# Second layer: where each attention row is divided by its mass

## The chip, the cores and the metric

The kernel runs on one NeuronCore of one Trainium2 chip. The metric is the device time of one execution in microseconds (us). Five engines work from queues of their own, each in the order of its program, and meet at semaphores: PE (TensorE, with its weight loads shown apart as PEld), DVE (VectorE), ACT (ScalarE), POOL (GpSimd) and SP (SyncE, which here issues the DMAs).

## What is computed

A graph of 1250 nodes with 512 features and 20000 edges goes through four layers. The second is a transformer of four blocks; each block has sparse attention with four heads of 128 features, written here densely over all 1250 x 1250 pairs with a matrix that holds the logarithm of the number of edges between two nodes, or -1e30 where there is none:

```python
for i in range(NUM_BLOCKS):                       # 4
    y = _cond_layer_norm(x, cond, s1_w[i], s1_b[i], b1_w[i], b1_b[i])
    # q, k, v = three projections of y, 4 heads each
    scores = jnp.einsum('ehd,ehd->eh', q[src], k[dst])
    smax = jax.ops.segment_max(scores, src, num_segments=N)
    ex = jnp.exp(scores - smax[src])
    denom = jax.ops.segment_sum(ex, src, num_segments=N)
    attn = ex / denom[src]
    y = jax.ops.segment_sum(attn[:, :, None] * v[dst], src, num_segments=N) @ wo + bo
    x = x + y
    # a second conditioned norm and a two-layer perceptron, added to x
```

## The kernel before

Nodes lie in 10 tiles of 125 rows. `second_layer` loops over the four blocks; inside, the attention loops over 4 heads and, in each, over steps i = 0 to 11, which hold tile i at one stage and earlier tiles at later ones. Every engine's queue is written out by hand in that loop, so the order of the code is the order of the work. For tile j of a head the stages are:

1. PE, `scores`: nine matmuls give the 125 x 1250 scores in PSUM (three for each of three column cuts, as queries and keys are split into a high and a low part). It waits until DVE has read the tile before (`scored`), since both use the same PSUM banks.
2. DVE, `row_scores` (L790, L794): adds the log counts, writes the row of scores to `prob` (two buffers) and its maximum.
3. ACT (L1248): the exponential in place, with the row sum (`fx.mass`).
4. DVE, `row_mass` (L800, L802): the inverse of the row sum.
5. PE, `turn` (L1087): ten 125 x 125 transposes of `prob` into PSUM in three units. It waits for the exponential (`exped`).
6. ACT (L1245) copies each unit to bf16 (`pt_h`), DVE (L1379) writes the rest of it as a second bf16 part (`pt_l`).
7. POOL (L941) puts the 125 inverse masses on the diagonal of a matrix, PE (`mass_on_rows`, L1096) multiplies it with ones so that every partition holds the inverse masses as a row, and ACT (L1257) copies two tiles of them to SBUF (`mass_rows`).
8. PE, `weighted` (15 matmuls a tile, a group of two tiles accumulating in one PSUM bank, `bank(5)`): values times turned probabilities. Before it starts a group it waits until DVE has read the one before (`o_done`).
9. DVE, `attend` (L1347): product of the group's 128 x 250 result and `mass_rows`.

In step i PE does `scores(i)`, `weighted(i-3)`, `turn(i-1)`, `mass_on_rows(i-2)`; ACT does the three copies of tile i-1 and then the exponential of tile i; DVE does `row_scores(i)`, `row_mass(i-1)`, the three `pt_l` of tile i-1 and, in even steps from 4 on, `attend`. Between two heads PE computes the next head's queries and keys (`project`, six products of 12 matmuls), with `turn(9)` after the first. In the last head of a block there is no next projection; there ACT and DVE also split the earlier heads' results (`attended_high`, `attended_low`, L1352) in steps 2 to 7. After the last `attend` of a block SP loads the block's input back, POOL adds a bias to it (L962) and DVE adds the output projection to it. POOL also splits the head weights (L894, L896) between its diagonals.

## Time and profile before

| | us |
|---|---|
| median of 3 runs | 2759.81 |
| lowest and highest | 2756.35 and 2760.05 |
| the profiled execution | 2755.59 |
| its span | 2753.6 |
| busy in the span: PE, DVE, ACT, POOL | 2383.1, 1724.6, 1009.4, 747.2 |

The span is the time from the first to the last instruction of the profiled execution; 2.0 us lie around it. Busy times are sums over stages with different limits, so the attention has to be read by itself: its first block lies between about 425 and 671 us of the span, and the other three repeat it, which makes about 980 us of the 2754.

### The profile page before, as it was taken

To read this page: it belongs to the slowest core of one execution; us is meant where nothing else is said; L and a number is where in the kernel's file an instruction comes from. 1 tells how busy PE (TensorE), PEld (TensorE's weight loads), DVE (VectorE), ACT (ScalarE), POOL (GpSimd) and SP (SyncE) were. 2 spreads that over 40 slices of the span, in tenths; PEclk is the share of its full clock that TensorE was granted. 3 is DMA by queue.
4 is the path that set the end of the run, shared out by engine and by line. 5 is a ranking of instruction groups with operands and counts; after the bars stand their busy time and mean duration, and the time that the engine had idled before them with its cause. 6 is when DMAs were issued, how large, how long until landed. Compare 5 with 4: busy or idle time off the path is not lost. (4 is left out here: it accounts for less than half of the span.)

```text
span 2753.6 us, 40835 instructions
## 1 busy us (share of the span) xinstructions
PE 2383.1 (87%) x14014; PEld 1794.2 (65%) x14014; DVE 1724.6 (63%) x3212; ACT 1009.4 (37%) x1746; POOL 747.2 (27%) x627
## 2 busy tenths in 40 slices
PE   6889879998888999788999798899987997888783
PEld 6884458887766888576888686788765553333331
DVE  8994355666654666644666655566663335899985
ACT  1123044445334555324555433454530032243342
POOL 0000051212532121533121344111160000366673
PEclk9999989999999999899999998999998997988887
DMA  1013020001101000201000210100024300000000
GB/s 61 30 44 95 22 74 9 9 9 52 41 21 50 9 13 5 86 24 47 9 9 9 68 37 27 36 9 9 24 95 144 81 9 19 0 0 0 1 0 37
DMA packets 67598, 91.20 MB, mean 33 GB/s; under 512 B 20485, under 2 KB 36869, under 8 KB 67377
## 3 DMA queue, kind: packets, MB, share of 16 engines
q1 hardware_dynamic: 67377, 88.41, 10.2%
q8 instruction: 120, 1.97, 0.3%
q14 instruction: 101, 0.83, 0.1%
HBM read 62.94 MB, written 25.45 MB: 32 GB/s over the span
## 5 line engine op out<-in xcount | busy, mean ns | idle before, releaser
L941 POOL TENSOR_SCALAR inverse_mass_diagonal<-identity,row_masses 125x125 f32<-125x125 f32 x160 | 96.8, 605 | 873.0 <-DVE row_masses L802 812.2
L1245 ACT ACTIVATE urned_probabilities_high<-psum 125x500 bf16<-125x500 f32 (+1 forms) x480 | 214.2, 521 | 251.5 <-PE psum L1087 251.5
L1379 DVE TENSOR_TENSOR turned_probabilities_low<-psum,urned_probabilities_high 125x500 bf16<-125x500 f32 (+1 forms) x480 | 254.3, 586 | 81.2 <-ACT urned_probabilities_high L1245 81.2
L790 DVE CUSTOM_DVE_ANT_0 probabilities<-psum,counts 125x1250 f32<-125x1250 f32 x160 | 233.5, 1459 | 103.3 <-PE psum L664 102.6
L1731 POOL TENSOR_TENSOR logs_and_shifts<-logs_by_source,target_spreads 125x1250 f32<-125x1250 f32 x80 | 217.4, 2722 | 156.4 <-DVE probabilities_turned L1804 88.5
L1950 PE MATMUL psum<-probabilities_turned,values_and_ones 125*65 125x512 f32 (+1 forms) x480 | 212.5, 589 | 34.7 <-ACT probabilities_turned L1867 18.6
L1248 ACT ACTIVATE probabilities<-probabilities,row_peaks 125x1250 f32<-125x1250 f32 x160 | 215.6, 1348 | 69.9 <-DVE row_peaks L794 67.9
L662 PE MATMUL psum<-urned_probabilities_high,values_high 125*128 125x250 bf16 x800 | 217.5, 272 | 13.1 <-DVE attended_turned L1347 8.8
L664 PE MATMUL psum<-urned_probabilities_high,values_low 125*128 125x250 bf16 x800 | 215.0, 269 | 0.0
L663 PE MATMUL psum<-turned_probabilities_low,values_high 125*128 125x250 bf16 x800 | 214.7, 268 | 0.0
L1804 DVE SCALAR_TENSOR_TENSOR probabilities_turned<-target_spreads,source_bends,logs_and_shifts 125x1250 f32<-125x1250 f32 x80 | 202.5, 2537 | 18.2 <-POOL logs_and_shifts L1731 18.2
L662 PE MATMUL psum<-keys_high,queries_high 128*125 128x512 f32 (+1 forms) x480 | 183.1, 381 | 28.9 <-DVE row_peaks L790 23.1
L1087 PE MATMUL psum<-identity,probabilities 125*125 125x125 f32 x1600 | 201.4, 273 | 1.3 <-ACT probabilities L1248 1.3
L1087 PEld LDWEIGHTS psum<-identity,probabilities 125*125 125x125 f32 x1600 | 187.9, 188 | 4.5 <-DVE turned_probabilities_low L1379 2.4
L445 ACT ACTIVATE norm_std<-norm_moments,norm_eps 125x1 f32<-125x1 f32 x120 | 35.2, 294 | 406.9 <-DVE norm_moments L441 406.9
L1950 PEld LDWEIGHTS psum<-probabilities_turned,values_and_ones 125*65 125x65 f32 x480 | 68.4, 153 | 172.4 <-issue 140.7
L662 PE MATMUL psum<-turned_high,head_weights 128*128 128x500 f32 (+1 forms) x384 | 145.3, 378 | 33.9 <-DVE queries_low L1339 25.8
L663 PE MATMUL psum<-keys_low,queries_high 128*125 128x512 f32 (+1 forms) x480 | 170.0, 354 | 0.0
L664 PE MATMUL psum<-keys_high,queries_low 128*125 128x512 f32 (+1 forms) x480 | 169.5, 353 | 0.0
L1867 ACT ACTIVATE probabilities_turned<-probabilities_turned,score_columns 125x1250 f32<-125x1250 f32 x80 | 106.7, 1337 | 156.3 <-DVE probabilities_turned L1804 156.0
L662 PE MATMUL psum<-slot_b_high,turned_high 128*125 128x512 f32 x320 | 134.4, 420 | 30.8 <-DVE nodes L1395 18.2
L306 PE MATMUL psum<-onehot_band,onehot_source 125*125 x2200 | 137.5, 224 | 17.2 <-DVE onehot_band L261 16.4
(267 smaller groups left out, 5449.8 us busy)
## 6 DMA issues: line engine op xcount, KB each, us to landing
block_inputs_kept<-nodes SPq DMA_DIRECT2D x4, 2500.0 KB
nodes<-block_inputs_kept SPq DMA_DIRECT2D x8, 1250.0 KB
weight_stage<-in_L_gnn_m_w SPq DMA_DIRECT2D x32, 256.0 KB, 2.6
counts_kept<-counts_by_target_rows SPq DMA_DIRECT2D x10, 625.0 KB, 3.5
counts_by_target<-counts_kept SPq DMA_DIRECT2D x1, 6103.5 KB
logs_kept<-counts SPq DMA_DIRECT2D x1, 5468.8 KB
logs_by_source<-logs_kept SPq DMA_DIRECT2D x1, 4375.0 KB
weight_stage<-in_L_gnn_wv SPq DMA_DIRECT2D x16, 256.0 KB, 2.6
```

The source lines that it names most:

```text
L306: mm = pe.matmul(region(b)[:, k * 128:(k + 1) * 128], onehot[0:TILE, q, k * TILE:(k + 1) * TILE], station[0:TILE, bass.ds(at, 1), q, :, :] ...
L662: pe.matmul(out, lh, rh, start=first, stop=False, skip_group_check=True)
L663: pe.matmul(out, lh, rl, start=False, stop=False, skip_group_check=True)
L664: return pe.matmul(out, ll, rh, start=False, stop=last, skip_group_check=True)
L790: dve.tensor_tensor_reduce(prob[0:TILE, i % 2, :], scores, fx.count_src[0:TILE, i, 0:NODES], scale, MASKED, ALU.add, ALU.max, p[:, 0:1]).t ...
L1087: mm = pe.transpose(bank((3, 4, 7)[u])[0:TILE, cols(d - 4 * u)], prob[0:TILE, j % 2, cols(d)], fx.ident[0:TILE, 0:TILE])
L1245: nc.scalar.activation(dst, src, ACT.Copy).then_inc(pt_high, 1)
L1248: nc.scalar.activation(prob[0:TILE, i % 2, :], prob[0:TILE, i % 2, :], ACT.Exp, bias=fx.peak[0:TILE, i % 2, 1:2], accum_out=fx.mass[0:TILE ...
L1379: dve.tensor_tensor(dst, src, high, ALU.subtract).then_inc(pt_low, 1)
L1731: nc.gpsimd.tensor_tensor(offset[0:TILE, T % 2, :], lw.logs[0:TILE, j, :], shifts[0:TILE, h % 2, :], ALU.add).then_inc(offset_ready, 1)
L1804: dve.scalar_tensor_tensor(prob[0:TILE, T % 4, :], target[0:TILE, h % 2, :], bend[0:TILE, j, h:h + 1], offset[0:TILE, T % 2, :], ALU.max, ...
L1950: mm = pe.matmul(region(0)[0:WIDTH, a:z], values[0:TILE, j, h, :], prob[0:TILE, T % 4, a:z], start=(j == 0), stop=(j == TILES - 1))
```

## The change

In the attention of the second layer the inverse masses no longer travel to the result. DVE multiplies each row of `prob` by its own inverse mass, a number per partition, in place, before the transposes; `turn` waits for that (`scaled`) and not for the exponential. Stage 7 is gone with its buffers and semaphores, `attend` is a plain copy out of PSUM, and on DVE `row_mass(i-1)`, which now has three instructions, stands ahead of `row_scores(i)`.

```diff
@@ row_mass
             dve.reciprocal(m[:, 2:3], m[:, 1:2]).then_inc(inverted, 1)
+            dve.wait_ge(inverted, T + 1)
+            p = prob[0:TILE, i % 2, :]
+            dve.tensor_scalar(p, p, m[:, 2:3], None, ALU.mult).then_inc(scaled, 1)
@@ POOL, steps of a head
-                        if h > 0 or j >= 2:
-
-                            pool.wait_ge(rows_prod, T - 1)
-                        wait_apart(pool, fx, inverted, T + 1)
-                        nc.gpsimd.tensor_scalar(mass_diag[0:TILE, j % 2, :], fx.ident[0:TILE, 0:TILE],
-                                                fx.mass[0:TILE, j, 2:3], None, ALU.mult).then_inc(diagonal, 1)
@@ PE, turn
-                    pe.wait_ge(exped, 40 * b + 10 * h + j + 1)
+                    pe.wait_ge(scaled, 40 * b + 10 * h + j + 1)
@@ PE, steps of a head
-                        if i >= 2:
-                            mass_on_rows(h, i - 2)
@@ ACT, steps of a head
-                        if i >= 3 and i % 2 == 1:
-                            g = (i - 3) // 2
-                            act.wait_ge(rows_prod, 40 * b + 10 * h + 2 * g + 2)
...
-                            nc.scalar.activation(mass_rows[:, g % 2, :], bank(6)[:, 0:250],
-                                                 ACT.Copy).then_inc(rows_copied, 1)
@@ DVE, attend
-                    dve.wait_ge(rows_copied, 20 * b + 5 * h + g + 1)
-                    dve.tensor_tensor(attended[:, h, 250 * g:250 * g + 250], bank(5)[:, 0:250], mass_rows[:, g % 2, :],
-                                      ALU.mult).then_inc(o_done, 1)
+                    dve.tensor_copy(attended[:, h, 250 * g:250 * g + 250], bank(5)[:, 0:250]).then_inc(o_done, 1)
@@ DVE, steps of a head
+                        if 1 <= i <= TILES:
+                            row_mass(dve, i - 1, T - 1)
                         if i < TILES:
...
                             row_scores(dve, psum[0:TILE, 0:NODES], i, T, HDIM1 ** -0.5)
-                        if 1 <= i <= TILES:
-                            row_mass(dve, i - 1, T - 1)
```

The queue of DVE in one even step from the middle of a head, before: the last `pt_l` of a tile, `attend`, and then the next step.

```order
L1379 TENSOR_TENSOR turned_probabilities_low<-psum,turned_probabilities_high 125x2x125
L1347 TENSOR_TENSOR attended_turned<-psum,inverse_mass_rows 128x250
L433 REGISTER_ALU
L790 ISA probabilities,row_peaks<-psum,counts 125x1250
L790 ISA row_peaks 125x1
L794 TENSOR_SCALAR row_peaks<-row_peaks 125x1
L800 TENSOR_SCALAR row_masses<-row_masses 125x1
L802 RECIPROCAL row_masses<-row_masses 125x1
L1376 REGISTER_ALU
L1379 TENSOR_TENSOR turned_probabilities_low<-psum,turned_probabilities_high 125x4x125
```

The same place of DVE's queue with the change (L786 is `row_scores`, L796 to L801 `row_mass`, L1320 `attend`, L1351 `pt_l`):

```order
L1351 TENSOR_TENSOR turned_probabilities_low<-psum,turned_probabilities_high 125x2x125
L1320 COPY attended_turned<-psum 128x250
L796 TENSOR_SCALAR row_masses<-row_masses 125x1
L798 RECIPROCAL row_masses<-row_masses 125x1
L801 TENSOR_SCALAR probabilities<-probabilities,row_masses 125x1250
L433 REGISTER_ALU
L786 ISA probabilities,row_peaks<-psum,counts 125x1250
L786 ISA row_peaks 125x1
L790 TENSOR_SCALAR row_peaks<-row_peaks 125x1
L1348 REGISTER_ALU
L1351 TENSOR_TENSOR turned_probabilities_low<-psum,turned_probabilities_high 125x4x125
```

The two instructions on the masses moved ahead of the scores of the next tile, with the 125 x 1250 product of the row behind them.

The queue of PE at the end of a step before, from the last matmul of `weighted` through `turn` to `scores`:

```order
L664 MATMUL psum<-turned_probabilities_high,values_low 128x250
L1085 REGISTER_ALU
L1087 MATMUL psum<-identity,probabilities 125x125 x4
L1085 REGISTER_ALU
L1087 MATMUL psum<-identity,probabilities 125x125 x4
L1085 REGISTER_ALU
L1087 MATMUL psum<-identity,probabilities 125x125 x2
L1096 MATMUL psum<-inverse_mass_diagonal,all_ones 128x125
L1059 REGISTER_ALU
L662 MATMUL psum<-keys_high,queries_high 125x512
```

And with the change (L1079 is `turn`):

```order
L1077 REGISTER_ALU
L1079 MATMUL psum<-identity,probabilities 125x125 x4
L1077 REGISTER_ALU
L1079 MATMUL psum<-identity,probabilities 125x125 x4
L1077 REGISTER_ALU
L1079 MATMUL psum<-identity,probabilities 125x125 x2
L1051 REGISTER_ALU
L662 MATMUL psum<-keys_high,queries_high 125x512
```

The one product between the transposes and the next scores is gone; nothing else on PE moved.

## Rows read from the trace of the kernel before

**Rows 1.** Stretches: start:end and length, each engine's busy us, granted clock, DMA.
```profile
425.00:671.00 246.00, 234.14 (x1661) 205.33 (x1659) 160.64 (x362) 131.10 (x248) 43.64 (x58) 1.00 0.04 11
```
**Rows 2.** Page, groups of instructions: busy us, mean ns, idle before and its releaser.
```profile
L941 POOL TENSOR_SCALAR inverse_mass_diagonal<-identity,row_masses 125x125 f32<-125x125 f32 x160 | 96.8, 605 | 873.0 <-DVE row_masses L802 812.2
```
**Rows 3.** Timeline of PE, one step of the first head: start us, duration, instruction.
```profile
447.00 0.27 PE L662 MATMUL psum<-urned_probabilities_high,values_high 125*128 125x250 bf16 x1
...
448.61 1.25 PE L1087 MATMUL psum<-identity,probabilities 125*125 125x125 f32 x10
449.70 0.39 PE L1096 MATMUL psum<-inverse_mass_diagonal,all_ones 125*128 125x125 f32 x2
449.84 0.50 PE L662 MATMUL psum<-keys_high,queries_high 128*125 128x512 f32 x1
...
451.70 0.28 PE L662 MATMUL psum<-urned_probabilities_high,values_high 125*128 125x250 bf16 x1
```
**Rows 4.** Timeline of DVE in the same step (idle before and releaser in brackets).
```profile
446.45 0.41 DVE L1347 TENSOR_TENSOR attended_turned<-psum,inverse_mass_rows 128x250 f32<-128x250 f32 x1
447.08 1.46 DVE L790 CUSTOM_DVE_ANT_0 probabilities<-psum,counts 125x1250 f32<-125x1250 f32 x1 [0.22 <-PE psum L664]
...
448.58 0.15 DVE L794 TENSOR_SCALAR row_peaks<-row_peaks 125x1 f32<-125x1 f32 x1
448.65 0.14 DVE L800 TENSOR_SCALAR row_masses<-row_masses 125x1 f32<-125x1 f32 x1
448.83 0.16 DVE L802 RECIPROCAL row_masses<-row_masses 125x1 f32<-125x1 f32 x1
449.87 1.59 DVE L1379 TENSOR_TENSOR turned_probabilities_low<-psum,urned_probabilities_high 125x500 bf16<-125x500 f32 x3 [0.87 <-ACT urned_probabilities_high L1245]
```
**Rows 5.** Timeline of ACT in the same step.
```profile
449.24 1.34 ACT L1245 ACTIVATE urned_probabilities_high<-psum 125x500 bf16<-125x500 f32 x3 [2.27 <-PE psum L1087]
450.45 1.35 ACT L1248 ACTIVATE probabilities<-probabilities,row_peaks 125x1250 f32<-125x1250 f32 x1
451.69 0.21 ACT L1248 ACTIVATION_READ_ACCUMULATOR probabilities<-probabilities,row_peaks 125x1 f32 x1
```
**Rows 6.** One line's instructions: DVE, a product with a number per partition.
```profile
L565 DVE TENSOR_SCALAR noise_phase<-noise_phase,lane_number x1: 864/864/864, 211.7 to 211.7; 64x1250 f32<-64x1250 f32 x1
```
**Rows 7.** Timeline of ACT and PE: the last transposes of a block.
```profile
660.27 0.21 ACT L1248 ACTIVATION_READ_ACCUMULATOR probabilities<-probabilities,row_peaks 125x1 f32 x1
...
660.61 1.35 PE L1087 MATMUL psum<-identity,probabilities 125*125 125x125 f32 x10 [0.33 <-ACT probabilities L1248]
...
661.34 1.07 ACT L1245 ACTIVATE urned_probabilities_high<-psum 125x500 bf16<-125x500 f32 x2 [0.59 <-PE psum L1087]
```
**Rows 8.** Timeline of DVE: scores, tiles 0, 1, 3, 9, next head's 0.
```profile
426.52 1.46 DVE L790 CUSTOM_DVE_ANT_0 probabilities<-psum,counts 125x1250 f32<-125x1250 f32 x1 [2.24 <-PE psum L664]
...
430.21 1.46 DVE L790 CUSTOM_DVE_ANT_0 probabilities<-psum,counts 125x1250 f32<-125x1250 f32 x1 [2.03 <-PE psum L664]
...
437.62 1.46 DVE L790 CUSTOM_DVE_ANT_0 probabilities<-psum,counts 125x1250 f32<-125x1250 f32 x1 [0.27 <-PE psum L664]
...
466.29 1.46 DVE L790 CUSTOM_DVE_ANT_0 probabilities<-psum,counts 125x1250 f32<-125x1250 f32 x1 [0.23 <-PE psum L664]
...
489.64 1.46 DVE L790 CUSTOM_DVE_ANT_0 probabilities<-psum,counts 125x1250 f32<-125x1250 f32 x1 [2.41 <-PE psum L664]
```
**Rows 9.** Timeline of DVE, last head: scores (tiles 0, 9), one split.
```profile
615.74 1.46 DVE L790 CUSTOM_DVE_ANT_0 probabilities<-psum,counts 125x1250 f32<-125x1250 f32 x1 [2.41 <-PE psum L664]
...
650.32 1.45 DVE L1352 TENSOR_TENSOR turned_low<-attended_turned,turned_high 128x1250 fp32r<-128x1250 f32 x1
...
655.61 1.46 DVE L790 CUSTOM_DVE_ANT_0 probabilities<-psum,counts 125x1250 f32<-125x1250 f32 x1 [0.17 <-PE psum L664]
```
**Rows 10.** Waits: who waited for whom, us in total, times, longest.
```profile
POOL nodes L962 <- DMA nodes<-block_inputs_kept: 52.7, 8, 8.1
```
**Rows 11.** One line's instructions: DVE copies of 1000 numbers a partition.
```profile
L1406 DVE CAST turned_high<-hidden_rows x20: 680/682/1747, 734.7 to 2077.7; 128x1000 fp32r<-128x1000 f32 x20
```

More of the change, by code:

```diff
@@ L701, in second_layer @@
         pt_l = place("turned_probabilities_low", [128, 2, TILES, 250], BF16)
-        mass_rows = place("inverse_mass_rows", [128, 2, 250], F32)
-        mass_diag = place("inverse_mass_diagonal", [128, 2, TILE], F32)
         hw = packer(nc, HEADW_AT)("head_weights", [128, 2, 2, CHUNKS, HDIM1], F32R)
@@ L749, in second_layer @@
         inverted = sem("inverted")
-        diagonal = sem("diagonal")
-        rows_prod = sem("rows_prod")
-        rows_copied = sem("rows_copied")
+        scaled = sem("scaled")
         turned = sem("turned")
@@ L912, in _ @@
                 pool.wait_ge(fx.counts_kept[k], 8 * GROUPS0)
-            pool.memset(raw[:, :, :], 0.0).then_inc(w_ready, 1)
-            pool.memset(mass_diag[0:1, 0, 0:1], 0.0).then_inc(w_ready, 1)
+            for k in range(2):
+                pool.memset(raw[:, k, :], 0.0).then_inc(w_ready, 1)
             pool.wait_ge(w_ready, 2)
@@ L935, in _ @@
                     for j in range(TILES):
-                        T = 40 * b + 10 * h + j
-                        if h > 0 or j >= 2:
-                            pool.wait_ge(rows_prod, T - 1)
-                        wait_apart(pool, fx, inverted, T + 1)
-                        nc.gpsimd.tensor_scalar(mass_diag[0:TILE, j % 2, :], fx.ident[0:TILE, 0:TILE],
-                                                fx.mass[0:TILE, j, 2:3], None, ALU.mult).then_inc(diagonal, 1)
                         if h < HEADS1 - 1 and j in (3, 6):
@@ L950, in _ @@
                         pool.wait_ge(mod_ready, 20 * b + 10)
-                        pool.wait_ge(diagonal, 40 * b + 20)
+                        pool.wait_ge(w_ready, 24 * b + 12)
                         condition(b, 1)
@@ L1089, in turn @@
                         mm.then_inc(turned, 1)
-                def mass_on_rows(h, j):
-                    pe.wait_ge(diagonal, 40 * b + 10 * h + j + 1)
-                    if j % 2 == 0 and (h > 0 or j > 0):
-                        pe.wait_ge(rows_copied, 20 * b + 5 * h + j // 2)
-                    pe.matmul(bank(6)[:, cols(j % 2)], fx.ones[0:TILE, :], mass_diag[0:TILE, j % 2, :], start=True,
-                              stop=True, skip_group_check=True).then_inc(rows_prod, 1)
                 project(0, range(6))
@@ L1250, in _ @@
                                                  accum_out=fx.mass[0:TILE, i, 0:1]).then_inc(exped, 1)
-                        if i >= 3 and i % 2 == 1:
-                            g = (i - 3) // 2
-                            act.wait_ge(rows_prod, 40 * b + 10 * h + 2 * g + 2)
-                            if h > 0 or g >= 2:
-                                act.wait_ge(o_done, 20 * b + 5 * h + max(g - 1, 0))
-                            nc.scalar.activation(mass_rows[:, g % 2, :], bank(6)[:, 0:250],
-                                                 ACT.Copy).then_inc(rows_copied, 1)
                         if not more and i in (2, 4, 6):
```

## The prediction

> **What bounds the kernel now.** First the busy time by stretches. In the first block's attention, 246.0 us, PE is busy 234.1, DVE 160.6, ACT 131.1 and POOL 43.6, at a granted clock of 1.00 [rows 1]. PE sets the pace there, and a quarter to a third of DVE's time is free. Then the groups: POOL's diagonals are 160 instructions, and POOL idled 873 us before them [rows 2]; POOL is late for nobody. Then one step of the middle of a head, engine by engine. On PE `weighted` takes 447.00 to 448.61 (1.61 us), `turn` to 449.70 (1.09), the spread product to 449.84 (0.14 to 0.15) and the next scores to 451.70 (1.86), 4.70 in all [rows 3]. DVE has gaps of 0.22 and 0.87 in the same step [rows 4], ACT one of 2.27 [rows 5]. The scores of DVE show the step: 3.69 us at the start of a head (426.52 to 430.21), then from tile 3 to tile 9 (437.62 to 466.29) 28.67 for six, 4.78 each [rows 8]. So on paper the change takes work from the engine that is full and gives it to one that is not. What decides is whether the work given lies inside a loop in which each tile waits for the one before.
>
> **What is removed.** On PE, 160 products (two overlapping passes each, 0.39 us together [rows 3]); what they occupy of the queue is 0.15 us each: 24 us, all of it in the queue that sets the pace. On ACT, 80 copies of 128 x 250 numbers (about as long as `attend`, which has that size), in its gap of 2.27 [rows 5]. On POOL 160 instructions of 0.605 us, which nobody waited for [rows 2]. `attend` was 0.41 us [rows 4]; it reads the same 250 numbers from PSUM as a copy and I leave it at 0.41. These three give nothing.
>
> **What is added.** On DVE 160 products of 125 x 1250 with a number per partition, in place in SBUF. The nearest row is the same operation over 1250 numbers, 0.864 us [rows 6], on 64 partitions. I take 0.864. Copies of 1000 numbers take 0.68 at best [rows 11], so below 0.80 I see nothing; the upper bound is 1.46, a pass over 1250 numbers with two sources [rows 4]. Busy time of DVE rises by 138 us. The Trainium skill gives a lower price ("VectorE: DVE Perf Modes", the section on the TRN2 errata): 58 cycles and half the elements at 0.96 GHz for such an operation, an estimate of 0.71 us. No row here of this form is as short, so the measured 0.864 stays; at 0.71 the sum below would be some 28 us and not 41.
>
> **The loop that it closes.** Before, `turn(i-1)` needed the exponential of tile i-1, and the scores of tile i on DVE needed nothing of it. Now both stand behind the scaled row. From one scaled row to the next:
> - to the transposes 0.12 to 0.14, I take 0.12: from the end of the sum at 660.48 to 660.61 on PE [rows 7]; between `attend` and PE it is 446.86 to 447.00, 0.14 [rows 3, 4];
> - transposes to the first copy on ACT 0.73, as PE was waiting (660.61 to 661.34) [rows 7]; 0.63 if it was not (448.61 to 449.24) [rows 3, 5];
> - three copies 1.21, exponential with its sum 1.45 (449.24, 450.45, 451.90) [rows 5];
> - to the maximum 0.03, maximum and inverse 0.34 (448.65 to 448.99) [rows 4], to the product 0.03 (as the gap ahead of the inverse, 448.79 to 448.83), product 0.86.
>
> That is 4.77 us. PE's own work without the spread product is 4.70 - 0.15 = 4.55 [rows 3]. So the loop, not PE, sets the step, by a narrow margin.
>
> **Heads 1 to 3 of a block.** First step: scores to exponential 1.69 (447.08 to 448.73 [rows 4] and a hop as from the sum to DVE), 1.45, then 0.03 + 0.34 + 0.03 + 0.80 until DVE can start the next scores: 4.34, where it was 3.69. Four steps at 4.77 follow, 19.1. From the first `attend` on, a pair of steps has a longer path: scores until the low parts 1.58, low parts 1.50, `attend` to `weighted` 0.55 (446.45 to 447.00), `weighted` 1.61, then 0.63 + 1.21 + 1.45 + 0.03 + 0.34 + 0.03 + 0.80 = 9.73; two pairs, 19.5. Sum 42.9 from tile 0 to tile 9, where it was 39.77 (426.52 to 466.29) [rows 8]: +3.1. Between heads PE is free of the loop, as a projection stands ahead of `turn(9)`; it has run ahead of DVE by 4.77 - 3.70 = 1.07 and is rid of three spread products, 0.44: the 23.35 us to the next head [rows 8] become 21.8. Net +1.6 a head, +4.8 for three.
>
> **Last head.** 615.74 to 655.61 was 39.87 [rows 9]. Here DVE also makes the splits of 1.45 us [rows 9] in three of the steps, and is full: 1.58 + 1.50 + 1.37 + 0.34 + 0.03 + 0.80 = 5.6 and 4.77 in turn, three times 10.4, behind 4.34 + 2 x 4.77: 45.1. +5.2. Behind tile 9 the transposes came 5.00 after the scores (655.61 to 660.61); now 0.17 + 0.73 + 1.21 + 1.45 + 0.03 + 0.34 + 0.03 + 0.86 + 0.12 = 4.94. No change. What follows hangs on the last `attend`: POOL waits for the DMA of the block's input [rows 10], which starts then, so a delay is passed on whole.
>
> **Sum.** 4.8 + 5.2 = 10.0 a block, and 0.3 for what the last head adds where a late `turn` also delays the low parts; four blocks make 41. The profiled execution of 2755.6 becomes 2797; the median of the runs shown lies 4.2 above it, so I forecast 2801 us. With the product at 0.80 and the hop to PE at 0.05 the block costs 8.7, hence 2791 from the lowest run shown; with 1.0 us for the product, or 0.1 to 0.15 more at the hops, 14, hence 2816 from the highest.
>
> **Rivals.**
> - PE stays the bound and the change gains. The mechanism is the full queue of PE without its 24 us. It decides if the loop closes in 4.55, so if product and hops are together 0.22 shorter than I have them. Even then the head starts cost, as they wait for an exponential and have no PE work to hide it; with those free too it would be 2760 - 23 = 2737. For it: PE's 95% (234.1 of 246.0). Against it: rows at hand for every link. 3%.
> - The same condition, but the starts and the last head still cost: with 0.60 for the product I get about 4.6 us a block, 2778. 6%. Something between, no measurable difference, 3%.
> - The product runs at the rate of a two-source pass, 1.46: 0.6 more in each of 160 steps and in DVE's full last head, 30 a block, 2880. Against it: the row of 0.864 is of that form. 3%.
> - DVE and POOL get in each other's way. The same copy of 1000 numbers takes 0.68 in the median and 1.75 at worst [rows 11]. If that strikes the added product, each strike lengthens the loop by up to 1.1. POOL has six weight splits and three condition copies left a block; nine strikes would be 10 a block, 2841. But POOL is no longer paced by the masses and makes the splits as soon as a head's projections are done, ahead of the first scaled row; I expect one strike a block. 5%. The Trainium skill ("SBUF", the section on SBUF's two separate sides) has a rule for such strikes: a VectorE operation in a two-port mode and a GpSimd operation lock a shared port pair for a whole instruction each. By it the added product, as a two-port operation, can be held for one GpSimd instruction, which is the case above and not the sum; the 1.75 agrees with it.
>
> **How the numbers follow.** Forecast 2801, 80%; 2791 to 2816 is its own range. Between it and the rivals lie a shorter loop than I could bound and a second or third strike a block, so I take 2785 to 2818. A measurement of this kernel tells 0.2%, 5.5 us, from no change. Faster by more: 3%. Within: 3%. Slower: 94%.
>
> **What would show it.** The added product near 0.86 us. DVE's scores 4.3 and then 4.8 apart at the start of a head in place of 3.7, some 42.8 from tile 0 to 9, and 63.1 from head to head become 64.7; in the last head 45. PE waiting for the scaled row ahead of `turn`, above 1 us in the first two steps. A median clock as before. Wrong would be: a step of 4.65 or less in the middle of a head (PE still the bound), a product above 1 us, or long records of it while POOL works.

## The result, and the profile after

The changed kernel takes 2822.19 us in the median of 4 runs (2814.84 to 2825.84), the kernel before 2758.08 (2755.59 to 2760.05). The ratio is 1.023, with a 95% interval of 1.0206 to 1.0253: 64 us slower. I had forecast 2801 and a range of 2785 to 2818, so the direction was right and the result lies above the range. The change cost half as much again as my sum.

In the page of the profiled run of after (2825.84 us) these lines answer to [rows 1] and [rows 2]: busy times over the whole span, the groups of the added product and of the transposes that now wait for it (the last column is idle time before them, and who ended it).

```profile
span 2823.6 us, 39591 instructions
...
PE 2414.8 (86%) x13694; PEld 1781.5 (63%) x13694; DVE 1870.7 (66%) x3372; ACT 984.6 (35%) x1666; POOL 649.0 (23%) x467
...
L1079 PE MATMUL psum<-identity,probabilities 125*125 125x125 f32 x1600 | 213.1, 281 | 63.0 <-DVE probabilities L801 62.3
...
L801 DVE TENSOR_SCALAR probabilities<-probabilities,row_masses 125x1250 f32<-125x1250 f32 x160 | 146.9, 918 | 5.6
```

DVE is busy for 146 us more than before (1870.7 for 1724.6). The transposes idle 63.0 us, 62.3 of it on the scaled row; before it was 1.3 us. The product's mean is 918 ns. Its own line shows that this is no typical value (minimum, median, maximum):

```profile
L801 DVE TENSOR_SCALAR probabilities<-probabilities,row_masses x160: 871/872/2715, 432.4 to 2040.5; 125x1250 f32<-125x1250 f32 x160
```

Nearly all take 0.872 us, and four, one in each block, take 2.71. One step in the middle of a head, as in [rows 3 to 5], here in the timelines of after (start, duration, instruction). DVE:

```profile
446.78 0.87 DVE L801 TENSOR_SCALAR probabilities<-probabilities,row_masses 125x1250 f32<-125x1250 f32 x1
447.57 1.46 DVE L786 CUSTOM_DVE_ANT_0 probabilities<-psum,counts 125x1250 f32<-125x1250 f32 x1
...
450.67 0.41 DVE L1320 COPY attended_turned<-psum 128x250 f32<-128x250 f32 x1
451.20 0.15 DVE L796 TENSOR_SCALAR row_masses<-row_masses 125x1 f32<-125x1 f32 x1
451.39 0.16 DVE L798 RECIPROCAL row_masses<-row_masses 125x1 f32<-125x1 f32 x1
451.59 0.87 DVE L801 TENSOR_SCALAR probabilities<-probabilities,row_masses 125x1250 f32<-125x1250 f32 x1
```

ACT in the same step:

```profile
448.52 1.34 ACT L1227 ACTIVATE urned_probabilities_high<-psum 125x500 bf16<-125x500 f32 x3 [2.16 <-PE psum L1079]
449.73 1.36 ACT L1230 ACTIVATE probabilities<-probabilities,row_peaks 125x1250 f32<-125x1250 f32 x1
450.96 0.21 ACT L1230 ACTIVATION_READ_ACCUMULATOR probabilities<-probabilities,row_peaks 125x1 f32 x1
```

And PE:

```profile
447.79 1.35 PE L1079 MATMUL psum<-identity,probabilities 125*125 125x125 f32 x10
```

Follow the loop: product 446.78 to 447.65, transposes 0.14 later, first copy 0.73 behind them, exponential 1.21 behind that, its sum done at 451.17, the masses at 451.20, the next product at 451.59. That is 4.81 us, where I had put 4.77.

The time is best split in three: **attention** (from the first scores of a block on DVE to the last, four blocks), **tails** (from the last scores to the last split of `attended_low`, L1352 before and L1324 after; four), and the **rest** of the span. All are differences of start times in the timelines.

| profiled run of | span | attention | tails | rest | median of its runs |
|---|---|---|---|---|---|
| before | 2753.6 | 916.4 | 54.2 | 1783.0 | 2758.08 |
| after | 2823.6 | 966.0 | 64.3 | 1793.3 | 2822.19 |
| e1_condition_held | 2814.9 | 956.3 | 63.3 | 1795.3 | 2812.50 |
| e2_tail_filled | 2809.6 | 965.7 | 54.3 | 1789.7 | 2812.16 |
| e3_held_and_filled | 2792.4 | 956.2 | 54.3 | 1781.9 | 2794.88 |
| e4_half_row | 2772.7 | 926.5 | 54.3 | 1791.9 | 2774.05 |
| e6_no_product | 2740.8 | 900.9 | 55.6 | 1784.3 | 2744.09 |
| e7_before_attend_early | 2744.6 | 908.2 | 52.6 | 1783.8 | 2749.27 |
| e12_after_again | 2813.2 | 965.2 | 63.8 | 1784.3 | 2818.14 |
| e13_both_again | 2792.7 | 956.3 | 54.2 | 1782.2 | 2795.94 |

After against before: 49.6 in the attention, 10.1 in the tails, 10.3 in the rest. My sum held 40 in the attention, about 1 for low parts that come late in the last head, and none in the tails. Two places in the trace of after have the remainder.

**The second head of each block.** From tile 0 to tile 9 the heads of the first block take 42.99, 45.75, 42.91 and 45.35 us. The second is the odd one. At its start DVE's timeline shows:

```profile
497.06 2.71 DVE L801 TENSOR_SCALAR probabilities<-probabilities,row_masses 125x1250 f32<-125x1250 f32 x1
499.69 1.45 DVE L786 CUSTOM_DVE_ANT_0 probabilities<-psum,counts 125x1250 f32<-125x1250 f32 x1
```

POOL's at that time:

```profile
495.65 1.03 POOL L903 CAST condition_weight_parts<-condition_weights 32x1024 fp32r<-32x1024 f32 x1 [0.17 <-POOL condition_weight_parts L901]
496.77 2.33 POOL L906 TENSOR_TENSOR condition_weight_parts<-condition_weights,condition_weight_parts 32x1024 fp32r<-32x1024 f32 x1
```

And PE's, with the transposes that wait for this product and the first matmul of the next scores:

```profile
499.90 2.46 PE L1079 MATMUL psum<-identity,probabilities 125*125 125x125 f32 x10 [2.90 <-DVE probabilities L801]
502.02 0.77 PE L662 MATMUL psum<-keys_high,queries_high 128*125 128x512 f32 x1
```

POOL's third condition copy (L906) runs from 496.77 to 499.10, and the product that starts inside it takes 2.71 us. PE waits 2.90 us for it and then does the transposes in 2.46 us and not in 1.25 to 1.35: its granted clock is 0.50 in that stretch, the lower of its two levels (1.2 and 2.4 GHz). The first step of this head is 6.17 us for 4.33 in the third head, and the second 5.67 for 4.81: the hold is 1.84 us of that, and the other 0.87 come in the step with the lower clock.

That the copies stand there at all comes from the change, by a line that the diff above leaves out. In the kernel before, POOL began `condition(b, 1)` only when it had made the diagonals of two heads (`pool.wait_ge(diagonal, 40 * b + 20)`), and its third copy ran at 537.96, behind the last scores of the second head. The change put `pool.wait_ge(w_ready, 24 * b + 12)` in its place, and the copy now runs at the start of that head.

**The tail.** PE waits about 2 us twice in it, ahead of the last transposes and ahead of `weighted(8)`, and after the second wait three matmuls of `weighted` take 0.62 us (679.13 to 679.73 and on) where they took 0.32 (PE's timeline):

```profile
675.81 1.35 PE L1079 MATMUL psum<-identity,probabilities 125*125 125x125 f32 x10 [1.85 <-DVE probabilities L801]
679.13 0.39 PE L662 MATMUL psum<-urned_probabilities_high,values_high 125*128 125x250 bf16 x1 [1.98 <-DVE attended_turned L1320]
679.32 0.41 PE L663 MATMUL psum<-turned_probabilities_low,values_high 125*128 125x250 bf16 x1
679.52 0.41 PE L664 MATMUL psum<-urned_probabilities_high,values_low 125*128 125x250 bf16 x1
679.73 0.41 PE L662 MATMUL psum<-urned_probabilities_high,values_high 125*128 125x250 bf16 x1
```

In the kernel before, the first of these waits was 0.33 us [rows 7] and the second 1.62, and behind it three matmuls took 0.32 (664.02 to 664.34):

```profile
664.02 0.27 PE L662 MATMUL psum<-urned_probabilities_high,values_high 125*128 125x250 bf16 x1 [1.62 <-DVE attended_turned L1347]
664.12 0.27 PE L663 MATMUL psum<-turned_probabilities_low,values_high 125*128 125x250 bf16 x1
664.23 0.27 PE L664 MATMUL psum<-urned_probabilities_high,values_low 125*128 125x250 bf16 x1
664.34 0.27 PE L662 MATMUL psum<-urned_probabilities_high,values_high 125*128 125x250 bf16 x1
```

The stretch of the tail, from the last scores to the end of the last split (length, busy times of PE, PEld, DVE, ACT, POOL, granted clock, DMA), lies at a clock of 1.00 in the kernel before:

```profile
655.61:670.60 14.99, 11.25 (x92) 9.60 (x92) 7.53 (x16) 8.26 (x16) 4.57 (x5) 1.00 0.23 60
```

And at 0.80 in after:

```profile
670.72:688.15 17.43, 11.77 (x77) 9.09 (x74) 8.18 (x16) 7.74 (x14) 3.38 (x3) 0.80 0.17 51
```

### The profile page after: what moved, and what is told of

Its sections match the earlier page's. It is cut to its first block and busy times, and to the rows that moved or that the text cites. A ratio compares the mean times of both kernels' runs of the same rounds, so it can differ in the third digit from the quotient of the medians.

```text
span 2823.6 us, 39591 instructions
## 1 busy us (share of the span) xinstructions
PE 2414.8 (86%) x13694; PEld 1781.5 (63%) x13694; DVE 1870.7 (66%) x3372; ACT 984.6 (35%) x1666; POOL 649.0 (23%) x467
## 5 line engine op out<-in xcount | busy, mean ns | idle before, releaser
L1079 PE MATMUL psum<-identity,probabilities 125*125 125x125 f32 x1600 | 213.1, 281 | 63.0 <-DVE probabilities L801 62.3
L1351 DVE TENSOR_TENSOR turned_probabilities_low<-psum,urned_probabilities_high 125x500 bf16<-125x500 f32 (+1 forms) x480 | 254.6, 587 | 8.8 <-ACT urned_probabilities_high L1227 7.1
L786 DVE CUSTOM_DVE_ANT_0 probabilities<-psum,counts 125x1250 f32<-125x1250 f32 x160 | 232.6, 1454 | 37.7 <-PE psum L664 37.7
L1922 PE MATMUL psum<-probabilities_turned,values_and_ones 125*65 125x512 f32 (+1 forms) x480 | 222.6, 613 | 33.5 <-ACT probabilities_turned L1839 17.0
L1079 PEld LDWEIGHTS psum<-identity,probabilities 125*125 125x125 f32 x1600 | 190.1, 190 | 85.8 <-issue 79.6
L306 PE MATMUL psum<-onehot_band,onehot_source 125*125 x2200 | 138.4, 224 | 17.0 <-DVE onehot_band L261 16.1
L801 DVE TENSOR_SCALAR probabilities<-probabilities,row_masses 125x1250 f32<-125x1250 f32 x160 | 146.9, 918 | 5.6
```

Of the source, the lines that this page charges most:

```text
L786: dve.tensor_tensor_reduce(prob[0:TILE, i % 2, :], scores, fx.count_src[0:TILE, i, 0:NODES], scale, MASKED, ALU.add, ALU.max, p[:, 0:1]).t ...
L801: dve.tensor_scalar(p, p, m[:, 2:3], None, ALU.mult).then_inc(scaled, 1)
L1079: mm = pe.transpose(bank((3, 4, 7)[u])[0:TILE, cols(d - 4 * u)], prob[0:TILE, j % 2, cols(d)], fx.ident[0:TILE, 0:TILE])
L1351: dve.tensor_tensor(dst, src, high, ALU.subtract).then_inc(pt_low, 1)
L1922: mm = pe.matmul(region(0)[0:WIDTH, a:z], values[0:TILE, j, h, :], prob[0:TILE, T % 4, a:z], start=(j == 0), stop=(j == TILES - 1))
```

## The experiments

**Theory.** The loop that the product closes costs 40 us, POOL's copy 10 and the lower clock of the tail 10. **Rival one:** the two places are by-products, and the heads or the rest would give the time back if they were mended. **Rival two:** what lies above my sum is in the rest of the program, through a clock that the change disturbs everywhere.

### The condition copies held back

POOL begins `condition(b, 1)` only when the rows of two heads are scaled, as late as in the kernel before; its third copy then runs at 544.09, behind the last product of the second head.

```diff
                         pool.wait_ge(w_ready, 24 * b + 12)
+                        pool.wait_ge(scaled, 40 * b + 20)
                         condition(b, 1)
```

> The changed kernel, with one wait added on POOL: the three copies of the second condition weights wait until the rows of the second head are scaled (as they did in the kernel before, by the diagonals). Theory A (POOL's third copy, 2.33 us, holds DVE's added product of the second head's first tile, which then takes 2.71 us for 0.87, and the wait lets TensorE's clock fall for the next 2.5 us): all 160 products between 0.86 and 0.90 us, second head of a block 43.0 us from tile 0 to tile 9 and not 44.9 to 45.8, so 9.7 us less over four blocks: 2812. Rival B (the long record is a slip of the profile, or the strike moves to another tile): second head unchanged or another head longer, 2822.

Measured 2812.50 us (2806.56 to 2816.79), a ratio of 1.0194 [1.0177, 1.0211]. The second head is 43.04 us instead of 45.75, and no product is long:

```profile
L801 DVE TENSOR_SCALAR probabilities<-probabilities,row_masses x160: 871/872/875, 432.4 to 2033.4; 125x1250 f32<-125x1250 f32 x160
```

The attention falls by 9.7 us in the profiled runs, and the median by 9.7 too. The heads do not give it back, which is against rival one. The tails stay at 15.66 to 15.91.

### The waits of the tail filled

Useless transposes of the identity into a free PSUM bank stand in both waits of the last head; nothing reads them.

```diff
+                        if not more and i == TILES:
+                            fill(14)
                         if 1 <= i <= TILES:
                             turn(h, i - 1)
...
                     if more:
                         project(h + 1, range(2, 6))
+                    else:
+                        fill(14)
                     weighted(h, TILES - 2)
```

> The changed kernel, with work without use on TensorE: in the last head of each block 14 transposes of the identity into the free bank 6 ahead of the last tile's transposes and 14 ahead of the product of tile 8, about 1.5 us each, in waits of 2.0 to 2.1 us. Theory A (the two waits let the granted clock fall to half, so the last products of a block run at 0.625 us for three matmuls and not 0.32): from the last scores to DVE's last split 13.6 us and not 15.8 to 16.3, so 9 us less over four blocks: 2813. Rival B (the end of the block is late through the loop itself, as the added product stands in it, and TensorE's clock plays no part): no change, 2822, or later by what the useless work delays.

Measured 2812.16 us (2809.99 to 2816.34), 1.0203 [1.0186, 1.022]. Work was added to PE and the tail became shorter, 13.57 us in every block, as before the change (13.55). What had made it longer was the clock and not something that has to be done there.

### Both together

> Both edits of the two runs above together. If the two causes are apart, the gains add: 19 us less than the changed kernel, 2803, and what is left over the kernel before is the loop alone: 12.9 us at heads 1 to 3 together less 8.1 given back between heads, and 5.5 in the last head, 10 a block, 40 in all, so 2798 and a few us that differ from run to run with the clock elsewhere. Rival: the gains overlap (one lowered clock leads to the other) and it stays at 2812.

Both edits of above in one kernel: 2794.88 us (2792.12 to 2803.64), 1.0145 [1.0124, 1.0167]. The trace is the one that I had predicted: heads of 42.97, 43.04, 42.89 and 45.34 us (forecast 42.9 and 45.1), 39.8 us more attention than before (forecast 40), tails as before. The medians differ by 37.4 us.

### Half a row scaled

e3_held_and_filled with the product over 625 of the 1250 columns. The other half stays undivided, so this kernel leaves out part of the computation.

```diff
-            p = prob[0:TILE, i % 2, :]
+            p = prob[0:TILE, i % 2, 0:625]
             dve.tensor_scalar(p, p, m[:, 2:3], None, ALU.mult).then_inc(scaled, 1)
```

> As the run above, but the added product covers 625 of the 1250 numbers of a row; the other half stays unscaled, so the output is another. The product should take 0.55 us for 0.87. Theory A (the added product lies in a loop from tile to tile that sets the step as long as it is over TensorE's 4.5 us): steps at a head's start 4.0 and 4.46 for 4.34 and 4.80, in the middle of a head TensorE sets the step again at 4.5 and, where it waits for the attended result, 4.9; 7.6 us a block, 30 us less than the run above: 2773. Rival B (VectorE's load in all sets the time): the gain is 160 x 0.33 = 52 us, 2751. Rival C (the order of DVE's queue costs, not the product): no gain, 2803.

Measured 2774.05 us (2772.74 to 2776.83), 1.0063 [1.0046, 1.008]. The product takes 0.546 us, 0.326 less. Single steps fall from 4.80 to 4.48 us, by 0.32: the product lies on the loop in its full length. If the price is linear between these two lengths, which is an estimate from two points, it is 0.22 us that do not depend on the length, and 0.52 ns a column. The paired steps fall by no more than that (4.95 + 4.80 to 4.95 + 4.48), so the attention gains 29.7 us and not 160 x 0.326 = 52.

### The product left out

e3_held_and_filled without the product: `turn` waits for the inverse masses only. The division is left out of the computation.

```diff
-            dve.reciprocal(m[:, 2:3], m[:, 1:2]).then_inc(inverted, 1)
-            dve.wait_ge(inverted, T + 1)
-            p = prob[0:TILE, i % 2, :]
-            dve.tensor_scalar(p, p, m[:, 2:3], None, ALU.mult).then_inc(scaled, 1)
+            dve.reciprocal(m[:, 2:3], m[:, 1:2]).then_inc(scaled, 1)
```

> The changed kernel with POOL's copies held and the useless transposes at the end of a block, and without the added product: the output lacks the division by the masses. The transposes wait for the inverse alone. Theory A (the product is the whole cost, and the removed product on TensorE is a gain where TensorE sets the step): steps at a head's start 3.7, 3.7, 3.9, then 4.5 and 4.9 in turn; 226 us a block from first to last scores, 3 less than in the kernel before: 2746. Theory B (the order, mass ahead of scores, costs by itself, as the scores wait for the exponential): steps of 4.0 at a head's start and a time at or above that of the kernel before, 2757 to 2765.

Measured 2744.09 us (2742.69 to 2745.32), 0.9955 [0.994, 0.997]. This is the most that the change could have brought had its product cost nothing: 14 us, and not the 24 us by which PE's queue became shorter. Where the other 10 are can be seen in the steps. The single steps in the middle of a head fall from 4.66 to 4.43 us and the gaps between heads from 23.35 to 22.35. But the steps that `attend` bounds stay (4.98 and 4.92 become 4.92 and 4.95), the third step of a head grows from 3.70 to 3.90, the wide steps of the last head grow from 5.73 to 5.86, and the tails are 1.4 us longer in all. So the first head gains only 0.5 us (39.27 for 39.77), and the last loses 0.6 (40.43 for 39.87). PE ahead of the transposes of tile 1 waits 0.26 us for the masses at the start of a head, where before it did not wait:

```profile
434.31 1.35 PE L1077 MATMUL psum<-identity,probabilities 125*125 125x125 f32 x10 [0.26 <-DVE row_masses L798]
```

### The scores ahead of the product

After with the old order on DVE: `row_scores(i)` and behind it the three instructions of `row_mass(i-1)`.

```diff
-                        if 1 <= i <= TILES:
-                            row_mass(dve, i - 1, T - 1)
                         if i < TILES:
...
                             row_scores(dve, psum[0:TILE, 0:NODES], i, T, HDIM1 ** -0.5)
+                        if 1 <= i <= TILES:
+                            row_mass(dve, i - 1, T - 1)
```

> The changed kernel with the old order on VectorE: the scores of tile i first, then mass, inverse and added product of tile i-1. The same instructions and the same load. Theory A (what counts is where the product stands in the loop): the transposes of tile i-1 wait for the scores of tile i and then the product, and the next scores on TensorE for the transposes: 1.6 + 0.35 + 0.87 + 0.13 + 1.09 + 2.16, with hops a step of 6.3 us, 294 us a block from first to last scores and not 241.5, 210 us more: 3035. Theory B (VectorE's load of about 4.6 us a step sets the time): no difference, 2822.

One run, 3088.12 us, 330 us above before and 53 above what I expected. The step was right: from one row of transposes to the next it is 6.20 and 6.22 us in the middle of the first head. The first steps were not. PE waits 3.1 us in each of them, and the transposes behind such a wait take 2.46 us; behind a wait of 1.5 us they take 1.35 (PE's timeline):

```profile
433.22 2.46 PE L1079 MATMUL psum<-identity,probabilities 125*125 125x125 f32 x10 [3.07 <-DVE probabilities L801]
...
440.86 2.46 PE L1079 MATMUL psum<-identity,probabilities 125*125 125x125 f32 x10 [3.15 <-DVE probabilities L801]
...
449.63 1.35 PE L1079 MATMUL psum<-identity,probabilities 125*125 125x125 f32 x10 [1.47 <-DVE probabilities L801]
...
455.83 1.35 PE L1079 MATMUL psum<-identity,probabilities 125*125 125x125 f32 x10 [1.52 <-DVE probabilities L801]
```

The heads are 55.9 to 57.5 us and the last 62.0, the gaps between them 24.2 (21.6 in after) and the tails 18.7 to 18.9 (16.1). Twelve gaps by 2.6 and four tails by 2.8 are 42 us that I had not put in: a loop that is entered later also lengthens what stands behind it. The move of the masses ahead of the scores, which looked like a detail of the change, keeps 266 us away.

### The condition copy in two halves

After, with POOL's third condition copy as two instructions of 512 numbers each.

```diff
-                nc.gpsimd.tensor_tensor(sw[32:64], raw[:, :, :], sw[0:32].bitcast(F32), ALU.subtract).then_inc(conds_ready, 1)
+                nc.gpsimd.tensor_tensor(sw[32:64, 0], raw[:, 0, :], sw[0:32, 0].bitcast(F32), ALU.subtract)
+                nc.gpsimd.tensor_tensor(sw[32:64, 1], raw[:, 1, :], sw[0:32, 1].bitcast(F32), ALU.subtract).then_inc(conds_ready, 1)
```

> The changed kernel with POOL's third copy of condition weights (2.33 us for 32 x 1024 numbers) made in two halves of about 1.2 us. Theory A (VectorE's added product is held until the instruction on POOL that began before it ends, and no longer): the long record, 2.71 us, becomes about 1.8 in each block (0.95 held, 0.87 of its own), second head 44.0 us for 45.5, and POOL's second half is held in turn. Rival B (POOL goes on and the product waits for both halves): 2.7 as before. 2822 or, by A, some 6 less.

One run, 2812.94 us. The longest product is now 1.64 us. In this kernel's timeline of DVE:

```profile
493.32 1.64 DVE L801 TENSOR_SCALAR probabilities<-probabilities,row_masses 125x1250 f32<-125x1250 f32 x1
```

And of POOL:

```profile
493.03 1.26 POOL L906 TENSOR_TENSOR condition_weight_parts<-condition_weights,condition_weight_parts 32x512 fp32r<-32x512 f32 x1
494.25 1.83 POOL L907 TENSOR_TENSOR condition_weight_parts<-condition_weights,condition_weight_parts 32x512 fp32r<-32x512 f32 x1
```

The product does not run slowly beside POOL, it waits for the end of the instruction that had begun: it ends 0.67 us after POOL's (494.96 against 494.29), and in after also 0.67 (499.77 against 499.10), although one copy is 1.85 times as long as the other. POOL's second half is then held in its turn, 1.83 us against the 1.26 of the first. The second head takes 43.89 to 44.05 us, up to 1.0 more than with the copies held back and not 2.7. The Trainium skill ("SBUF — State Buffer", the section on SBUF's two separate sides) calls the port pair that the two engines share an exclusive lock, held for a whole instruction, and both traces agree with it: 0.67 us behind the other's end in each, whatever its length.

### One wait of the tail filled, and the other

These are e3_held_and_filled with `fill(14)` in the first wait alone, and in the second alone. They ask which wait lowers the clock.

> The kernel after with the third condition copy held back (as e1_condition_held, 2812.5 us, whose tail from the last scores to the last split is 15.7 to 15.9 us) and 14 useless transposes only in the first of the two waits of the last head, ahead of the last transposes; the second wait, about 2 us ahead of weighted(8), stays. Theory A, either wait alone lets the granted clock fall: the tail stays at 15.7 to 16. Theory B, it takes both: the tail is 13.6, as where both were filled, and the three matmuls of one step of weighted take 0.32 us. Theory C, the second wait alone does it: 15.7 to 16, and e10_second_gap then has 13.6. The time of one run scatters by 5 us, so the tail decides; whole time 2810 by A and C, 2800 by B.

> The counterpart of e9_first_gap: the 14 useless transposes only in the second wait, ahead of weighted(8); the first, about 2 us ahead of the last transposes, stays. Theory A (either wait is enough): tail 15.5 to 16, the slow matmuls perhaps earlier. Theory B (both are needed) and C (the second does it): tail 13.6. Whole time 2810 by A, 2800 by B and C.

One run each, 2806.41 and 2796.24 us. With the first filled the tails are 15.21, 13.56, 15.22 and 15.23; with the second filled 14.59, 14.58, 14.59 and 13.57. None of the three theories had that. A single wait of 1.8 to 2.0 us can lower the clock, in three blocks of four, and leaves it alone in the fourth, with the same work around it. In the first block of e9_first_gap the fall comes 0.9 us after the wait, inside `weighted` (PE's timeline):

```profile
672.39 0.28 PE L662 MATMUL psum<-urned_probabilities_high,values_high 125*128 125x250 bf16 x1 [1.97 <-DVE attended_turned L1329]
...
672.94 0.27 PE L664 MATMUL psum<-urned_probabilities_high,values_low 125*128 125x250 bf16 x1
...
673.27 0.41 PE L664 MATMUL psum<-urned_probabilities_high,values_low 125*128 125x250 bf16 x1
```

In the first block of e10_second_gap the transposes behind the first wait and the fillers run low, and `weighted` is fast again:

```profile
670.27 1.75 PE L1080 MATMUL psum<-identity,probabilities 125*125 125x125 f32 x10 [1.84 <-DVE probabilities L801]
671.82 2.98 PE L1086 MATMUL psum<-identity 125*125 125x125 f32 x14
674.84 0.27 PE L664 MATMUL psum<-urned_probabilities_high,values_low 125*128 125x250 bf16 x1
```

The same 14 fillers take 1.69 us at the full clock. In the second and third block of that run the transposes still run at the full clock (1.35 us) and the fall comes in the fillers (3.01). With both waits the tail was long in all eight blocks of the two profiled runs of after (15.79 to 16.37) and in the four of e1_condition_held (15.66 to 15.91). What decides whether the clock falls in a given block stays open.

### attend ahead of the low parts, before the change

This asks whether the step pairs are bound as I read them (`weighted` waits for `attend`, which stands behind the low parts). Only the order on DVE is changed, in even steps, in the kernel before:

```diff
                         if i < TILES:
                             ...
+                        if i >= 4 and i % 2 == 0:
+                            attend(h, (i - 4) // 2)
                         if 1 <= i <= TILES:
                             ...
-                        if i >= 4 and i % 2 == 0:
-                            attend(h, (i - 4) // 2)
```

> The kernel before, with one edit: in even steps VectorE reads the finished group (attend) ahead of the three low parts of tile i-1 and not behind them. There it has a gap of 0.87 us in which it waits for ScalarE's first copy, and the group is finished 0.3 us into it. Theory A (TensorE waits 0.25 to 0.3 us for it every second step, 4.90 to 4.98 against 4.65): these steps become 4.65, 0.25 x 2 or 3 in each of the first three heads, little in the last one where VectorE is full, 2.5 us a block: 2747. Rival (the low parts are then late for TensorE): no gain, 2757 or above.

Measured 2749.27 us (2746.59 to 2752.17, 8 runs) against 2758.20 of before, a ratio of 0.9971 [0.9961, 0.9982]. The steps of 4.90 to 4.98 have become 4.65 to 4.71, the first three heads 39.21 to 39.28 (39.67 to 39.79), gaps 23.14 (23.35), tails 13.15 (13.55): 9.8 us by the trace. It computes the reference in full, and it is faster than both kernels, by 0.3% against the one before.

### The same in the changed kernel

This is e3_held_and_filled with `attend` ahead of the low parts in even steps.

> e3_held_and_filled (2794.88 us) with attend ahead of the low parts in even steps. My theory is that pairs of steps are 9.75 us and not 9.60 because weighted(i-3) waits for attend, which stands behind the low parts; with attend ahead of them that path is 1.5 us shorter, so the loop of 4.80 alone is left: steps of 4.80 in place of 4.94 (three of them a head in three heads: 1.2 us a block), 0.2 us in each gap between heads and 0.4 in the tail, as e7_before_attend_early showed (gap 23.35 to 23.14, tail 13.55 to 13.15). Together about 2 us a block: 2787 us, range 2783 to 2791. Rival: the pair is bound by VectorE's own work, then the steps of 4.94 stay and only the tail's 0.4 a block comes: 2793.

Measured 2800.42 us (2798.26 to 2802.91), 1.0148 [1.0131, 1.0165]; e3_held_and_filled had 1.0145 [1.0124, 1.0167]. The gain of 8 us did not come. By its trace the attention is 954.7, 1.5 us less than without the move, and the tails are 53.5, 0.8 less; the rest of its profiled run is 1793.0, 11.1 more than in e3_held_and_filled, so the medians can't show a gain this small. The paired steps went from 4.95 to 4.83 us in the first two heads, but grew from 4.87 to 4.94 in the third, and the wide steps of the last head from 5.68 to 5.74. In the first two heads the path through `attend` was real, and the loop of 4.80 stood right behind it. Why the third and the last head lose by the move is not shown; the low parts, which stand ahead of the next masses in either order, are 0.3 us later by it.

### The rest of the program: both kernels again

After, and e3_held_and_filled, once more and unaltered.

> The changed kernel once more, unaltered, beside e13_both_again on one chip. Its first traced run has 35.1 us added inside the span, to 966.0 from 916.4 in the attention and to 64.3 from 54.2 in the four tails, 59.7 in all, and 10.3 more in the rest of the program, which the change does not touch. By median it was 64.1 us above before, so 4.4 are in the rest. Theory S (scatter): the rest differs from run to run with the granted clock and has nothing to do with the change; then the difference to e13_both_again is what the traces account for, 9.8 in the attention and 10.1 in the tails, 20 us, within 3. Theory R: the lower clock in the tails or the shifted times cost something elsewhere in every run; then the difference is 25 to 29, as it was between the first medians (2822.2 and 2794.9).

> e3_held_and_filled once more, unaltered, on the same chip as e12_after_again. Its first median was 37.4 us above before, where its traces add 39.8 in the attention and nothing in the tails. Theory S: 39.8 above before within 3, so about 2798, and 20 below e12_after_again. Theory R: again about 37 above before, and 25 to 29 below e12_after_again.

(The 35.1 in the first of these texts is a slip: the span rose by 70.0, which is 49.6 + 10.1 + 10.3.) On one chip, in five rounds, after takes 2818.14 us (2815.45 to 2820.37; 1.022 [1.0206, 1.0234]) and the mended one 2795.94 (2794.56 to 2797.72; 1.0138 [1.0123, 1.0154]), beside 2758.03 for before. They differ by 22.2 us, and the traces account for 18.5 (965.2 + 63.8 against 956.3 + 54.2). After lies 60.1 us above before, where its trace gives 58.4 for attention and tails (the first gave 59.7); the mended one lies 37.9 above, where its trace gives 39.9. This time the rest of after is 1784.3 us, within 1.3 of before's 1783.0, so the 10.3 us in the first profiled run did not belong to the change. Most of them, 7.5, lie behind the last block, in a stretch that the change does not touch: it took 763.9 us in before at a granted clock of 0.87, 771.4 in after at 0.85, and 766.2 in e12_after_again at 0.87, with 1986 matmuls in each. Rival two is not borne out: nothing that repeats is left for it beyond 2 us.

## Why the prediction was right, and where it was wrong

The direction, the loop and its 40 us were right. The forecast missed at two of its terms: the meeting of the added product with POOL, which it expected and left out of the sum, and the end of a block, which it put at no change. They cost 9.7 and 10.1 us.

- **The product at 0.864.** 0.872, in 160 instructions. Right; so was the choice against the lower price of 0.71. The copy in `attend` at 0.41 us was 0.409.
- **The loop at 4.77 and its links.** 4.81 in the step shown above, 4.80 in most. e4_half_row moved the step by the same 0.32 us as the product. Right.
- **Heads.** First step 4.34, measured 4.33. A pair 9.73, measured 4.95 + 4.80 in the first two heads and 4.87 + 4.80 in the third; that `attend` is on the path of a pair is shown for the first two only (e11_attend_early_after). Tile 0 to 9 in 42.9, measured 42.98. The gap of 21.8 to the next head was 21.64, the last head 45.35 for 45.1. In e3_held_and_filled these terms alone are left and add 39.8 us for my 40. Right, and shown.
- **The rival that PE's 24 us come in.** They do not: without the product at all, only 14 of them would (e6_no_product).
- **Wrong: "I expect one strike a block", at "up to 1.1" and left out of the sum.** There is one strike a block, where I put it, but it costs 2.7 us in the first block (45.75 for 43.04) and 9.7 in the four. The 1.1 came from the longest copy of [rows 11]. That row shows how long that copy happened to be held, not how long one can be; the bound was to be read from the longest POOL instruction that can run near the start of a head, and the trace of before had it: its third condition copy (L907) took 2.33 to 2.41 us. The product was held for 1.84, and the wait that this made on PE (2.90 us) lowered the clock for the transposes, 2.46 us for 1.35. Having written that I expected one a block, I should have had it in the sum. And "ahead of the first scaled row" was true for the weight splits alone: the condition copies stand behind them in POOL's queue. So "these three give nothing" did not hold for POOL: with its stage went the wait that had kept these copies out of the way.
- **Wrong: "Behind tile 9 ... No change", and "A median clock as before".** The chain was right: from the last scores to the last transposes 5.09 us for my 4.94. What I did not ask is what PE does meanwhile. Before, PE reached these transposes 0.33 us early, as it was behind; now it is done early and waits 1.85 us, and the second wait is 1.98 us for 1.62. The granted clock falls to its lower level for up to 5 us, and the tail is 2.5 us longer, 10.1 in four. With the waits filled the 10.1 us are gone (e2_tail_filled). Right duration of the chain, wrong price of the matmuls behind it.
- **The remainder.** The median was 64.1 above before; attention and tails have 59.7 of it, and a second set of runs gave 60.1. The 4 us between differ from set to set. In the ten profiled runs of the table the rest lies between 1781.9 and 1795.3, and in the three runs compared above most of that is a clock of 0.85 or 0.87 behind the last block; what sets it is open.
- **The range.** Its upper end had a second and third strike at 1.1 us and nothing for the clock. With the mended price of the strike (9.7) and nothing else the forecast would have been 2811, and with the tails (10.1) 2821.

## What to carry to other kernels

Work moved off the engine that is full, onto one that has time, is only free if it stays out of the loop in which each tile waits for the one before; add the links of the closed loop from rows and compare with the full engine's step, to a tenth of a microsecond. When a change turns the busiest engine into one that waits, price the waits of TensorE twice, once as time and once as the lower clock of the matmuls behind them. And price a meeting of VectorE with GpSimd by the longest GpSimd instruction that can be under way there. When a stage is taken out, look for every wait on its semaphores in other work: here such a wait was what kept the condition copies clear of the new product.

## What the runs showed of the hardware

- A single wait of TensorE of 1.84 to 1.97 us brought matmuls at the lower clock in six tails of eight (e9_first_gap, e10_second_gap). Waits of 1.47 and 1.52 us in e5_scores_first were followed by transposes of 1.35 us, and the 1.62 us in the tail of before left the granted clock at 1.00. Waits of 2.90 to 3.15 us did lower it at once in the three places shown, but behind a wait of 3.09 us at 689.41 in after the matmuls start at the full clock (0.40 us each) and fall to the lower one (0.63) 1.2 us later (PE's timeline, below). The fall may so come after the wait, in the middle of work. I had not expected that 2 us are enough, nor that the same place would differ from block to block.

```profile
689.41 0.49 PE L662 MATMUL psum<-slot_b_high,turned_high 128*125 128x512 f32 x1 [3.09 <-POOL slot_b_low L948]
689.74 0.40 PE L663 MATMUL psum<-slot_b_low,turned_high 128*125 128x512 f32 x1
...
691.00 0.63 PE L663 MATMUL psum<-slot_b_low,turned_high 128*125 128x512 f32 x1
```

- Fourteen useless transposes in each of the two waits cost nothing and took 2.5 us off a tail (13.57 us for 15.79 to 16.34). In a kernel whose waits can't be removed this is worth a trial.
- The VectorE product of an SBUF row ends 0.67 us after the end of the GpSimd instruction that it met, for a GpSimd instruction of 2.33 us as for one of 1.26, and the next GpSimd instruction was held in turn (1.83 us for 1.26, e8_copy_in_halves).
